# Product keys: which engine makes the pair sums of the last of eight heads

## The chip, the core and the metric

The kernel runs on one core of one Trainium2 chip. The metric is the device time of one execution in microseconds (us); the median of several runs counts.

## What is computed

The program is a stack of eight residual layers over x of 8 x 256 x 128 (2048 tokens of 128 channels); each adds its result to x, after a layer norm. The change touches the fourth, a product-key memory, which the reference writes so (cut):

```python
xn = (x - mean) * rsqrt(var + EPS) * bn_gamma + bn_beta           # over all tokens
q = (xn @ w_q.T).reshape(b, s, 2, NH, KD).transpose(2, 0, 1, 3, 4)
sim = einsum('pbnhd,hkpd->pbnhk', q, keys_p)                       # 2 halves x 8 heads x 32 keys
scores, idx = top_k(sim, K)                                        # K = 8 of each half
all_scores = scores[0][..., :, None] + scores[1][..., None, :]     # 8 x 8 pair sums
sc, pk = top_k(all_scores, K)                                      # the best 8 pairs
hmid = sigmoid(sc) * gelu(einsum('bnd,bnhkd->bnhk', inputs, down[indices]))
out = einsum('bnhk,bnhkd->bnd', hmid, up[indices])
```

A pair (i, j) of key indices names row 32 i + j of the tables `down` and `up`, so only the first 1024 rows are in play.

## The kernel before, in words

The tokens lie in 16 tiles of 128 (one token a partition). Each layer is a block in which every engine has its own instruction list; semaphores order them. Nothing is gathered in the product-key layer: for each of the eight heads the kernel writes out all 32 x 32 = 1024 pair sums of a token, and a threshold, the eighth best pair sum, decides which of them count.

Per tile n the work goes like this (function `product_keys`):

- **Half scores.** ScalarE applies the batch norm (`batch_normed`, L1495), TensorE multiplies by the folded query and key weights (`halves`, L1566), ScalarE copies the 512 half scores into one of two SBUF buffers `Ssb` (`store_s`, L1502). It does so for tile n+1 in the middle of tile n, after the sigmoid of head 3.
- **Pair sums.** GpSimd adds, head by head, the two halves into `A[h]`, 128 x 1024 fp32 in SBUF (L1541). One set of eight buffers `A` serves all tiles, so the sum of head h must wait until head h of the tile before has been turned by TensorE (semaphore `g_turned`), and all wait for `s_stored`. The semaphore `added` counts the sums.
- **Selection** (`picks`). VectorE finds the best 8 of each half with 16 max instructions (L1431), forms the 64 candidate sums of each head in one 128 x 512 addition (L1434; this is the "candidate sum"), and takes the best 8 of each head (L1438). It then adds the output of tile n-2 to x (`add_out`, L1452) and multiplies the turned gates of tile n-1 by the gelu values (`weigh`, the masking product, L1447).
- **Gates.** For head h ScalarE takes the sigmoid of all pair sums into one of two PSUM buffers `SG` (L1508), and VectorE multiplies it by the comparison of the pair sum with the threshold, in place in `A[h]` (L1463; these are the eight "products" of a tile). Its pair sums and thresholds come from SBUF, the sigmoid from PSUM.
- **Turn.** TensorE transposes the 1024 gates of each head in eight 128 x 128 pieces and adds the heads up in PSUM (`turn`, L1572).
- **Output.** TensorE multiplies the masked values by `up` (`output`, L1582). Beside this it projects x by `down` for the next block of four tiles (`project`, L1559), and ScalarE applies gelu (L1490).

The order on each engine is written out by hand in the `step` functions; the first four tiles are written out, the others run in a loop. ScalarE's order in a tile is: sigmoids 0 to 3, the store of the next tile's half scores, sigmoids 4 to 7, batch norm, two gelus. Sigmoid h waits for GpSimd's sum of its head and, through `g_ready`, for product h-2. The DMA queues are idle in this layer.

Of the kernel before, what the change touches and what calls it, by code (L numbers as in the profile page):

```python
# [20 lines left out]
ALU = mybir.AluOpType  # L21
# [19 lines left out]
NH, NK = 8, 32  # L41
# [30 lines left out]
def known(n, least):  # L72

    return not isinstance(n, int) or n >= least


def run_tiles(eng, step):


    for n in range(TPB):  # L80
        step(n, n, 0)
    with eng.Fori(1, NB - 1) as i:
        for r in range(TPB):
            step(i * TPB + r, r, i)
    for n in range(NT - TPB, NT):
        step(n, n % TPB, NB - 1)
# [90 lines left out]
def over(ap, axis, n):  # L177

    ap = ap.unsqueeze(axis)
    shape = list(ap.shape)  # L180
    shape[axis] = n
    return ap.broadcast_to(shape)
# [52 lines left out]
def norm_scalar(act, k, nm, first=None, high=None):  # L235

    act.wait_ge(nm.var_ready, 1)
    act.activation(k.mom[:, 6, :], k.mom[:, 4, :], ACT.Sqrt, bias=k.eps[:, 0:1],
                   scale=1.0 / D).then_inc(nm.std_ready, 1)
    if nm.turn:  # L240
        if first:
            first()
        for b in range(NB):
            act.wait_ge(nm.xt_turned, b + 1)
            act.activation(k.XT[:, bass.ts(b, BLK)], k.PS[:, b, :], ACT.Copy).then_inc(nm.xt_ready, 1)
            if high:
                high(act, b)
# [1117 lines left out]
def product_keys(k):  # L1365
# [8 lines left out]
    s = lambda what: k.sem(f"l1f_{what}")  # L1374
# [2 lines left out]
    bn_var, bn_std, bn_ready = s("bn_var"), s("bn_std"), s("bn_ready")  # L1377
    z_ready, z_stored = s("z_ready"), s("z_stored")
    xb_ready, s_ready, s_stored = s("xb_ready"), s("s_ready"), s("s_stored")
    added, sig_ready, g_ready, g_turned = s("added"), s("sig_ready"), s("g_ready"), s("g_turned")  # L1380
    m_ready, out_ready, out_added = s("m_ready"), s("out_ready"), s("out_added")

# [21 lines left out]
    def pair_scores(r, h):  # L1404
        s0 = over(Ssb[r][:, bass.ts(h, NK)], 2, NK)
        s1 = over(Ssb[r][:, bass.ts(NH + h, NK)], 1, NK)
        return A[h].rearrange("p (a b) -> p a b", a=NK), s0, s1

    with nc.Block() as block:

        @block.vector
        def _(dve):
            own = Tally(dve, vec)
            norm_vector(dve, k, nm, own)

            for q in range(NB):
                dve.wait_ge(nm.xt_ready, q + 1)
                own.mark(dve.bn_stats(bn[:, bass.ts(q, 6)], k.XT[:, bass.ts(q, BLK)]))
            own.wait()
            dve.bn_aggr(mv, bn[:, 0:24]).then_inc(bn_var, 1)  # L1420
            dve.wait_ge(bn_std, 1)
            own.settle(dve.reciprocal(brstd[:, 0:1], bstd[:, 0:1]))
            own.settle(dve.tensor_tensor(scale[:, 0:1], brstd[:, 0:1], k.col("gamma"), ALU.mult))
            own.settle(dve.tensor_tensor(tmp[:, 0:1], scale[:, 0:1], mv[:, 0:1], ALU.mult))
            dve.tensor_tensor(shift[:, 0:1], k.col("beta"), tmp[:, 0:1], ALU.subtract).then_inc(bn_ready, 1)

            def picks(n, r):
                dve.wait_ge(s_stored, n + 1)
                dve.sem_inc(paced, 1)
                for j in range(2 * NH):  # L1430
                    own.mark(dve.max(t8[:, j, :], Ssb[r][:, bass.ts(j, NK)]))  # L1431
                own.wait()

                own.settle(dve.tensor_tensor(cand.rearrange("p (h a b) -> p h a b", h=NH, a=8),  # L1434
                                             over(t8[:, 0:NH, :], 3, 8), over(t8[:, NH:, :], 2, 8), ALU.add))
                dve.sem_inc(paced, 1)
                for h in range(NH):
                    own.mark(dve.max(v8[:, h, :], cand[:, bass.ts(h, 64)]))  # L1438
                own.wait()

            def weigh(n, r, q):

                dve.wait_ge(g_turned, (n + 1) * NH)
                dve.wait_ge(z_stored, (q + 1) * 8)
                if known(n, 2):
                    dve.wait_ge(out_ready, n - 1)
                dve.tensor_tensor(M[r].rearrange("p (c t) -> p c t", c=8), gt.rearrange("p (c t) -> p c t", c=8),  # L1447
                                  zT[:, :, bass.ts(n, P)], ALU.mult).then_inc(m_ready, 1)

            def add_out(n):  # L1450
                dve.wait_ge(out_ready, n + 1)
                dve.tensor_tensor(k.X[:, n, :], k.X[:, n, :], PS[:, OUT, 0:D], ALU.add).then_inc(out_added, 1)  # L1452

            def step(n, t, q):
                r = t % 2
                picks(n, r)
                if known(n, 2):
                    add_out(n - 2)
                if known(n, 1):
                    weigh(n - 1, 1 - r, q if t else q - 1)  # L1460
                for h in range(NH):
                    dve.wait_ge(sig_ready, n * NH + h + 1)
                    dve.scalar_tensor_tensor(A[h], A[h], v8[:, h, 7:8], SG[h % 2], ALU.is_ge,  # L1463
                                             ALU.mult).then_inc(g_ready, 1)

            per = 2 * NH + 1 + NH
            for n in range(TPB):
                step(n, n, 0)
            with dve.Fori(1, NB) as i:
                own.enter(i - 1, TPB * per)  # L1470
                for t in range(TPB):
                    step(i * TPB + t, t, i)
            own.leave(NB - 1)
            add_out(NT - 2)
            weigh(NT - 1, 1, NB - 1)
            add_out(NT - 1)

        @block.scalar
        def _(act):
            act.wait_ge(wf_ready, 1)  # L1480
            act.activation(Wf, PS[:, WF, :], ACT.Copy).then_inc(wf_stored, 1)
            norm_scalar(act, k, nm)
            act.wait_ge(bn_var, 1)
            act.activation(bstd[:, 0:1], mv[:, 1:2], ACT.Sqrt, bias=k.eps[:, 0:1]).then_inc(bn_std, 1)
            act.wait_ge(bn_ready, 1)

            def gelu(m, c, q):

                act.wait_ge(z_ready, m + 1)
                act.activation(zT[:, c, bass.ts(q, BLK)], PS[:, Z + c % 2, :], ACT.Gelu).then_inc(z_stored, 1)  # L1490

            def batch_normed(n, r):
                if known(n, 2):
                    act.wait_ge(s_ready, n - 1)
                act.activation(xb[r], k.XT[:, bass.ts(n, P)], ACT.Identity, bias=shift[:, 0:1],  # L1495
                               scale=scale[:, 0:1]).then_inc(xb_ready, 1)

            def store_s(n, r):
                act.wait_ge(s_ready, n + 1)
                if known(n, 2):  # L1500
                    act.wait_ge(added, (n - 1) * NH)
                act.activation(Ssb[r], PS[:, SP, :], ACT.Copy).then_inc(s_stored, 1)  # L1502

            def sigmoid(n, h):
                act.wait_ge(added, n * NH + h + 1)
                if known(n, 1) or h >= 2:
                    act.wait_ge(g_ready, n * NH + h - 1)
                act.activation(SG[h % 2], A[h], ACT.Sigmoid).then_inc(sig_ready, 1)  # L1508

            def step(n, t, q):  # L1510
                r = t % 2
                for h in range(4):
                    sigmoid(n, h)
                if not isinstance(n, int) or n + 1 < NT:
                    store_s(n + 1, 1 - r)
                for h in range(4, NH):
                    sigmoid(n, h)
                if not isinstance(n, int) or n + 2 < NT:
                    batch_normed(n + 2, r)
                if not isinstance(n, int) or n + TPB < NT:  # L1520
                    for c in (2 * t, 2 * t + 1):
                        gelu(n * 2 + 8 + c % 2, c, q + 1)

            batch_normed(0, 0)
            batch_normed(1, 1)
            store_s(0, 0)
            for c in range(8):
                gelu(c, c, 0)
            run_tiles(act, step)

        @block.gpsimd
        def _(pool):
            k.clear_last(pool)

            def step(n, t, q):
                r = t % 2
                pool.wait_ge(s_stored, n + 1)
                for h in range(NH):
                    if known(n, 1):
                        pool.wait_ge(g_turned, (n - 1) * NH + h + 1)  # L1540
                    pool.tensor_tensor(*pair_scores(r, h), ALU.add).then_inc(added, 1)  # L1541
            run_tiles(pool, step)
# [634 lines left out]
```

## Time and profile before

| | us |
|---|---|
| median of 3 runs | 1546.37 (1543.95 to 1548.54) |
| the profiled execution, its own time | 1538.79 |
| span of its instructions | 1537.1 |
| busy: TensorE / VectorE / ScalarE / GpSimd | 1341.4 / 1054.2 / 936.5 / 878.9 |
| the product-key layer's tiles in it, first pair sum to last output add | about 387.7 to 647.8 |

The times in the rows below count from the start of the span. In a timeline a line is "start, duration, engine, line, operation, output <- inputs, shapes, count", and several like instructions in a row are one line; what stands in brackets is the idle time ahead of it and what ended it. PE is TensorE, PEld its weight loads, DVE VectorE, ACT ScalarE, POOL GpSimd. PEclk is the share of full speed that TensorE's clock was granted. RA holds the buffers `A`, RW the half scores and the candidates.

### The profile page before, as it was taken

The numbers are of one execution on the slowest core, as the hardware profiler recorded it, in microseconds if no ns is written. First come the engines' busy times: TensorE is split into PE (matmuls) and PEld (weight loads), VectorE is DVE, ScalarE is ACT, GpSimd is POOL, SyncE is SP. The second block draws the span as 40 slices with busy tenths as digits, with TensorE's granted clock in tenths as the row PEclk, the third lists the DMA queues.
The fourth block names the chain that finished last, engine by engine and source line by source line (L and its number), as shares of the span: only waits on it lengthen the run. The fifth ranks groups of instructions, "written<-read, shape, count | busy, mean of one in ns | idle before, by whom it ended". The sixth has DMA issues, their size and how long they took to land. (4 is left out here: it accounts for less than half of the span.)

```text
span 1537.1 us, 25078 instructions
## 1 busy us (share of the span) xinstructions
PE 1341.4 (87%) x8116; PEld 1040.6 (68%) x8116; DVE 1054.2 (69%) x2126; ACT 936.5 (61%) x1435; POOL 878.9 (57%) x619
## 2 busy tenths in 40 slices
PE   9789999797888887789489999998898349999998
PEld 8767777465466666646368887885787338787786
DVE  5534444597699999889756666673666766666665
ACT  4467787553787876477246765556665327555554
POOL 4168888300899999532047776661345128666655
PEclk9689999898899999899689999999999769999999
DMA  6021110000000000030044435332000135443442
GB/s 250 1 63 43 42 48 27 2 2 1 1 1 1 1 0 0 26 142 2 1 136 127 127 123 178 129 124 113 2 1 1 55 78 130 122 130 123 129 120 86
DMA packets 51561, 103.31 MB, mean 67 GB/s; under 512 B 6248, under 2 KB 10928, under 8 KB 49936
## 3 DMA queue, kind: packets, MB, share of 16 engines
q1 hardware_dynamic: 51472, 102.17, 21.6%
q8 instruction: 50, 0.82, 0.2%
q14 instruction: 39, 0.32, 0.1%
HBM read 99.99 MB, written 2.16 MB: 66 GB/s over the span
## 5 line engine op out<-in xcount | busy, mean ns | idle before, releaser
L1541 POOL TENSOR_TENSOR RA<-RW 128x1024 f32<-128x1024 f32 x128 | 246.7, 1965 | 86.1 <-ACT RW L1502 86.1
L881 ACT ACTIVATE PS<-PS 128x512 f32<-128x512 f32 (+1 forms) x260 | 151.1, 582 | 215.3 <-PE PS L677 214.6
L974 POOL TENSOR_TENSOR l3f_hid_rest<-RW,l3f_hid_high 128x512 fp32r<-128x512 f32 x132 | 170.5, 1292 | 141.3 <-ACT l3f_hid_high L873 141.3
L974 POOL TENSOR_TENSOR l2f_hid_rest<-RW,l2f_hid_high 128x512 fp32r<-128x512 f32 x128 | 165.3, 1292 | 136.9 <-ACT l2f_hid_high L873 136.9
L974 POOL TENSOR_TENSOR l0f_hid_rest<-RW,l0f_hid_high 128x512 fp32r<-128x512 f32 x128 | 165.2, 1292 | 64.7 <-ACT l0f_hid_high L873 56.4
L934 DVE TENSOR_TENSOR RW<-RW,PS 128x512 f32<-128x512 f32 (+1 forms) x260 | 178.7, 687 | 11.7 <-DVE RW L929 0.9
L1572 PE MATMUL PS<-identf,RA 128*128 128x128 f32 x1024 | 139.8, 287 | 37.0 <-DVE RA L1463 33.1
L1572 PEld LDWEIGHTS PS<-identf,RA 128*128 128x128 f32 x1024 | 118.1, 147 | 72.6 <-DVE RA L1463 69.3
L1463 DVE SCALAR_TENSOR_TENSOR RA<-RA,RW,PS 128x1024 f32<-128x1024 f32 x128 | 157.0, 1277 | 11.0 <-ACT PS L1508 10.4
L1508 ACT ACTIVATE PS<-RA 128x1024 f32<-128x1024 f32 x128 | 130.1, 1026 | 54.3 <-DVE RA L1463 51.8
L934 DVE TENSOR_TENSOR RW<-RD,PS 128x512 f32<-128x512 f32 x128 | 87.9, 687 | 108.3 <-ACT PS L881 99.9
L929 DVE TENSOR_TENSOR RW<-RB,PS 128x512 f32<-128x512 f32 x128 | 88.0, 688 | 92.1 <-PE PS L677 83.1
L929 DVE TENSOR_TENSOR RW<-RD,PS 128x512 f32<-128x512 f32 x128 | 87.9, 687 | 86.0 <-PE PS L677 73.9
L881 ACT ACTIVATE PS<-PS,cols 128x512 f32<-128x512 f32 x128 | 84.6, 662 | 37.6 <-PE PS L677 37.3
L675 PE MATMUL PS<-l3f_x_high,l3f_first_high 128*128 (+1 forms) x224 | 88.9, 397 | 9.7 <-DVE RW L934 9.6
L676 PE MATMUL PS<-l3f_x_rest,l3f_first_high 128*128 (+1 forms) x224 | 87.7, 392 | 0.0
L677 PE MATMUL PS<-l3f_x_high,l3f_first_rest 128*128 (+1 forms) x224 | 87.7, 391 | 0.0
L873 ACT ACTIVATE l3f_hid_high<-RW 128x512 fp32r<-128x512 f32 x132 | 82.4, 624 | 7.5 <-DVE RW L934 7.5
L873 ACT ACTIVATE l2f_hid_high<-RW 128x512 fp32r<-128x512 f32 x128 | 79.9, 624 | 8.8 <-DVE RW L934 8.7
L873 ACT ACTIVATE l0f_hid_high<-RW 128x512 fp32r<-128x512 f32 x128 | 79.8, 623 | 5.1 <-DVE RW L934 5.1
L274 PE MATMUL PS<-identf,XN 128*128 128x128 f32 x128 | 31.2, 398 | 39.5 <-DVE XN L231 39.5
L675 PE MATMUL PS<-l0f_hid_high,l0f_w_high 128*128 128x512 f32 x128 | 56.8, 443 | 6.1 <-POOL l0f_hid_rest L974 6.1
(339 smaller groups left out, 3346.4 us busy)
## 6 DMA issues: line engine op xcount, KB each, us to landing
RD<-l2f_kept SPq DMA_DIRECT2D x128, 256.0 KB, 3.5
RB<-l3f_kept SPq DMA_DIRECT2D x128, 256.0 KB, 3.7
RD<-l0f_kept SPq DMA_DIRECT2D x32, 256.0 KB, 3.1
RA<-in_w SPq DMA_DIRECT2D x2, 2048.0 KB, 10.0
RA<-in_wg SPq DMA_DIRECT2D x2, 1024.0 KB, 9.7
RA<-in_wu SPq DMA_DIRECT2D x2, 1024.0 KB, 11.7
RA<-in_wd SPq DMA_DIRECT2D x2, 1024.0 KB, 13.6
RC<-in_wg SPq DMA_DIRECT2D x1, 2048.0 KB, 8.5
```

Source lines behind the costliest of these rows:

```text
L675: pe.matmul(out, wh, xh, start=start, stop=False)
L676: pe.matmul(out, wh, xl, start=False, stop=False)
L677: return pe.matmul(out, wl, xh, start=False, stop=stop)
L873: act.activation(e.HIGH[c][0:st.rows, :], e.HID[c][0:st.rows, :], ACT.Copy).then_inc(e.rounded, 1)
L881: act.activation(gate, gate, e.func, bias=st.bias).then_inc(e.acted, 1)
L929: dve.tensor_tensor(product, factor, up, ALU.mult).then_inc(e.multiplied, 1)
L934: dve.tensor_tensor(place(e.HID, c, st), factor, PS[rows, e.GATE + c % e.gates, :], ALU.mult).then_inc(e.weighted, 1)
L974: pool.tensor_tensor(rest, hid, high, ALU.subtract).then_inc(e.hidden_ready, 1)
L1463: dve.scalar_tensor_tensor(A[h], A[h], v8[:, h, 7:8], SG[h % 2], ALU.is_ge, ALU.mult).then_inc(g_ready, 1)
L1508: act.activation(SG[h % 2], A[h], ACT.Sigmoid).then_inc(sig_ready, 1)
L1541: pool.tensor_tensor(*pair_scores(r, h), ALU.add).then_inc(added, 1)
L1572: mm = pe.matmul(gt[:, bass.ts(c, P)], A[h][:, bass.ts(c, P)], k.identf[:], start=(h == 0 and c % 4 == 0), stop=(h == NH - 1), is_transpos ...
```

## The change

The pair sums of the last head (h = 7) are taken off GpSimd's list, which makes seven per tile. VectorE makes them instead, between the products of heads 3 and 4 of the same tile, behind a wait for the turn of the previous tile's last head. A new semaphore `added_last` counts them; ScalarE's sigmoid 7 and its store of half scores wait for it, and the counts of `added` go by seven. The instruction is the same `tensor_tensor` addition with the same operands.

```diff
--- before.py
+++ after.py
@@ -1377,6 +1377,7 @@
     bn_var, bn_std, bn_ready = s("bn_var"), s("bn_std"), s("bn_ready")
     z_ready, z_stored = s("z_ready"), s("z_stored")
     xb_ready, s_ready, s_stored = s("xb_ready"), s("s_ready"), s("s_stored")
+    added_last = s("added_last")
     added, sig_ready, g_ready, g_turned = s("added"), s("sig_ready"), s("g_ready"), s("g_turned")
     m_ready, out_ready, out_added = s("m_ready"), s("out_ready"), s("out_added")
 
@@ -1459,6 +1460,10 @@
                 if known(n, 1):
                     weigh(n - 1, 1 - r, q if t else q - 1)
                 for h in range(NH):
+                    if h == NH // 2:
+                        if known(n, 1):
+                            dve.wait_ge(g_turned, n * NH)
+                        dve.tensor_tensor(*pair_scores(r, NH - 1), ALU.add).then_inc(added_last, 1)
                     dve.wait_ge(sig_ready, n * NH + h + 1)
                     dve.scalar_tensor_tensor(A[h], A[h], v8[:, h, 7:8], SG[h % 2], ALU.is_ge,
                                              ALU.mult).then_inc(g_ready, 1)
@@ -1498,11 +1503,15 @@
             def store_s(n, r):
                 act.wait_ge(s_ready, n + 1)
                 if known(n, 2):
-                    act.wait_ge(added, (n - 1) * NH)
+                    act.wait_ge(added, (n - 1) * (NH - 1))
+                    act.wait_ge(added_last, n - 1)
                 act.activation(Ssb[r], PS[:, SP, :], ACT.Copy).then_inc(s_stored, 1)
 
             def sigmoid(n, h):
-                act.wait_ge(added, n * NH + h + 1)
+                if h < NH - 1:
+                    act.wait_ge(added, n * (NH - 1) + h + 1)
+                else:
+                    act.wait_ge(added_last, n + 1)
                 if known(n, 1) or h >= 2:
                     act.wait_ge(g_ready, n * NH + h - 1)
                 act.activation(SG[h % 2], A[h], ACT.Sigmoid).then_inc(sig_ready, 1)
@@ -1535,7 +1544,7 @@
             def step(n, t, q):
                 r = t % 2
                 pool.wait_ge(s_stored, n + 1)
-                for h in range(NH):
+                for h in range(NH - 1):
                     if known(n, 1):
                         pool.wait_ge(g_turned, (n - 1) * NH + h + 1)
                     pool.tensor_tensor(*pair_scores(r, h), ALU.add).then_inc(added, 1)
```

## Rows read from the trace of the kernel before

**Rows 1.** Busy time by stretch: twelve tiles, then one tile.

```profile
core 0: us, PE busy (x) PEld busy (x) DVE busy (x) ACT busy (x) POOL busy (x), PEclk, DMA share, GB/s
440.00:631.00 191.00, 157.30 (x1048) 119.24 (x1046) 184.03 (x448) 144.95 (x161) 191.00 (x100) 0.98 0.00 1
507.74:523.36 15.62, 13.16 (x87) 9.57 (x86) 14.92 (x37) 12.60 (x14) 15.62 (x9) 1.00 0.00 1
```

**Rows 2.** Waits of VectorE in the same 191 us: total us, times, longest.

```profile
DVE RW L1438 <- DVE RW L1434: 1.7, 11, 0.2
DVE RA L1463 <- ACT PS L1508: 1.5, 10, 0.2
DVE X L1452 <- DVE RW L1438: 0.8, 3, 0.3
```

**Rows 3.** Timeline of one tile, VectorE and ScalarE: start us, us, what.

```profile
507.74 4.90 DVE L1463 SCALAR_TENSOR_TENSOR RA<-RA,RW,PS 128x1024 f32<-128x1024 f32 x4
511.26 0.58 ACT L1502 ACTIVATE RW<-PS 128x512 f32<-128x512 f32 x1
517.62 1.58 DVE L1431 MAX8 RW<-RW 128x8 f32<-128x32 f32 x16
519.23 1.07 DVE L1434 TENSOR_TENSOR RW<-RW 128x512 f32<-128x512 f32 x1
521.83 0.29 DVE L1452 TENSOR_TENSOR X<-X,PS 128x128 f32 x1 [0.25 <-DVE RW L1438]
523.36 4.90 DVE L1463 SCALAR_TENSOR_TENSOR RA<-RA,RW,PS 128x1024 f32<-128x1024 f32 x4
```

**Rows 4.** GpSimd sums (L1541) and VectorE's candidate sum (L1434): instructions in ns, then timelines.

```profile
L1541 POOL TENSOR_TENSOR RA<-RW x128: 1900/1910/2375, 387.7 to 633.7; 128x1024 f32<-128x1024 f32 x128
L1434 DVE TENSOR_TENSOR RW<-RW x16: 753/1028/1492, 389.4 to 627.1; 128x512 f32<-128x512 f32 x16
387.67 1.91 POOL L1541 TENSOR_TENSOR RA<-RW 128x1024 f32<-128x1024 f32 x1 [84.84 <-ACT RW L1502]
389.35 0.77 DVE L1434 TENSOR_TENSOR RW<-RW 128x512 f32<-128x512 f32 x1
425.33 1.92 POOL L1541 TENSOR_TENSOR RA<-RW 128x1024 f32<-128x1024 f32 x1
426.31 1.49 DVE L1434 TENSOR_TENSOR RW<-RW 128x512 f32<-128x512 f32 x1
427.19 2.38 POOL L1541 TENSOR_TENSOR RA<-RW 128x1024 f32<-128x1024 f32 x1
430.43 1.27 DVE L1463 SCALAR_TENSOR_TENSOR RA<-RA,RW,PS 128x1024 f32<-128x1024 f32 x1
```

**Rows 5.** Larger additions with two SBUF inputs: a group (mean ns), then a timeline.

```profile
L1033 DVE TENSOR_TENSOR RB<-RB 128x1024 f32<-128x1024 f32 x1 | 1.2, 1224 | 0.0
661.79 1.27 POOL L1268 TENSOR_TENSOR RB<-RB,vmask 128x512 f32<-128x512 f32 x1 [26.19 <-DVE RB L1170]
662.16 3.05 DVE L1174 TENSOR_TENSOR X<-X,rows 128x2048 f32<-128x2048 f32 x1
663.02 3.32 POOL L1268 TENSOR_TENSOR RB<-RB,vmask 128x512 f32<-128x512 f32 x1
```

**Rows 6.** Timeline of the first tile and of the last tile's products.

```profile
400.12 9.97 DVE L1463 SCALAR_TENSOR_TENSOR RA<-RA,RW,PS 128x1024 f32<-128x1024 f32 x8 [8.74 <-ACT PS L1508]
403.65 0.58 ACT L1502 ACTIVATE RW<-PS 128x512 f32<-128x512 f32 x1
404.31 1.92 POOL L1541 TENSOR_TENSOR RA<-RW 128x1024 f32<-128x1024 f32 x1 [1.21 <-ACT RW L1502]
631.07 9.77 DVE L1463 SCALAR_TENSOR_TENSOR RA<-RA,RW,PS 128x1024 f32<-128x1024 f32 x8
```

**Rows 7.** Busy time of a stretch with a lower granted clock, columns as above.

```profile
414.80:424.70 9.90, 8.56 (x58) 7.86 (x58) 9.75 (x10) 7.85 (x10) 9.90 (x6) 0.83 0.01 2
```

## The prediction

> **What bounds the kernel now.** The busy times by stretch come first. Over 191 us in the middle of the product-key stage, 12.4 tiles, GpSimd is busy for all 191.00 us and VectorE for 184.03, 96% [rows 1]. TensorE and ScalarE are at 82% and 76%. The reader is to see two engines at the limit, not one. A GpSimd sum takes 1910 ns in the median, and its neighbours overlap slightly: one starts at 425.33, its successor is recorded from 427.19, 1.86 later [rows 4]. Eight of them and one delay of 0.45 us, explained below, make 15.3 to 15.4 us. The first product of tile 0 starts at 400.12 and that of tile 15 at 631.07 [rows 6]: 230.95 / 15 = 15.40 us a tile. So GpSimd paces the stage, and its pace for one sum is (15.40 - 0.45) / 8 = 1.87 us.
>
> The waits come second: how much room has VectorE? In the same 191 us it waits 1.5 us for ScalarE's sigmoid, 1.7 us for its own previous result and 0.8 us in front of the output add [rows 2]. Per tile that is a third of a microsecond, and the 1.7 is a latency that nothing here removes. The timeline of one tile, third, shows VectorE's order with no other hole: eight products from 507.74, the selection from 517.62, the candidate sum at 519.23, the next tile's products at 523.36 [rows 3].
>
> **What is moved.** Per tile one 128x1024 sum leaves GpSimd (1.87 us of its pace) and comes to VectorE, between the fourth and fifth product; sixteen in all. No DMA is touched.
>
> *Its bare cost on VectorE.* This stage has no such sum there. The nearest row is the same operation, shape and type, both inputs in SBUF, in another layer: 1224 ns [rows 5]. Neighbours overlap a little, so one adds about 1.1 us.
>
> *Its wait.* The stage already holds one VectorE operation with two SBUF inputs, the candidate sum of 128x512 (L1434). It should cost the same each time, yet takes 753 to 1492 ns [rows 4]. The GpSimd sums beside it explain this. At 389.35 a GpSimd sum is running that ends at 387.67 + 1.91 = 389.58; VectorE ends at 390.12, 0.54 later. At 426.31 the running sum ends at 427.25, and VectorE ends at 427.80, 0.55 later [rows 4]. VectorE's operation gets nowhere until the running GpSimd sum ends, then needs 0.55 us. The next GpSimd sum, recorded from 427.19, takes 2.38 us instead of 1.91: it waits in turn, which is the 0.45 above. A larger case agrees: a 128x2048 add that starts at 662.16 under a GpSimd operation ending at 663.06 ends at 665.21, 2.15 later, and the next GpSimd operation takes 3.32 us where the one before took 1.27 [rows 5]. From 512 to 2048 elements the part behind the wait goes from 0.55 to 2.15, so 1024 elements take 0.55 + 512 x 1.60 / 1536 = 1.08 us. The products have one SBUF input and don't show this: four take 4.90 us beside GpSimd, eight 9.77 in the last tile, half of it without GpSimd [rows 3, 6].
>
> The Trainium skill bears on this: the page "Advanced Engine Details and Errata", section "VectorE Performance Modes", says that the second Vector SBUF port is shared, so that GpSimd and two-port Vector instructions block each other, and the page "VectorE: DVE Perf Modes", section "Mode 2×_2P — use both read ports for one tensor", says that tensor_tensor cannot use that mode. Taken to the letter nothing would block here, and the time would be the first rival's. The rows above speak against the letter. "GPSIMD Engine Reference", section "Key points", counts two SBUF inputs as a case too; with that the trace agrees.
>
> *Where GpSimd stands when the new sum comes.* Count from a tile's first product, t = 0. ScalarE stores the next tile's half scores from 511.26 to 511.84, until t = 4.10 [rows 3]. If GpSimd is idle then, it starts 0.08 us later (ScalarE ends at 404.23, GpSimd starts at 404.31 [rows 6]), so its first sum runs from 4.18 to 6.09. VectorE's fourth product ends at 4.90 [rows 3]. So in every tile the new sum starts under that first sum, waits until 6.09 and ends at 6.09 + 1.08 = 7.17: about 2.3 us of VectorE's time, not 1.1. Behind it in the queue stand products 4 to 7 and the next selection; TensorE's turns and ScalarE's sigmoids 6 and 7 wait for these.
>
> *What follows in the tile.* The remaining products take 4.9 us, to 12.0; the selection starts at 11.95 and the candidate sum 1.61 later (517.62 to 519.23 [rows 3]), at 13.56. GpSimd's second sum was held up and ends 1.77 after VectorE lets go (the one from 427.19 ends at 429.57, VectorE had ended at 427.80 [rows 4]), at 8.94; the third, fourth and fifth end at 10.81, 12.68 and 14.55. The candidate sum therefore waits for the fifth and ends at 14.55 + 0.55 = 15.10. From its end to the next tile's first product it is 3.06 us in one tile (520.30 to 523.36 [rows 3]), which includes the 0.25 of wait in front of the output add, and 2.63 where the candidate sum was longest (427.80 to 430.43 [rows 4]). I take 2.85. The period is 15.10 + 2.85 = 17.95 us.
>
> Is GpSimd idle when I said so? Its seven sums start at 4.18 and need 7 x 1.87 + 0.45 + about 1.0 (the hold by the moved sum: midway by size between 0.45 and 3.32 - 1.27 = 2.05), to 18.7; its next start is at 17.95 + 4.18 = 22.1. Yes, for 3.4 us. Its work is then hidden; so is the 13.16 us of TensorE and the 12.60 of ScalarE in a tile [rows 1].
>
> *New waits, costed at nothing.* VectorE's wait for the turn of the previous tile's last head has been passed by its masking product, earlier in the same queue; without it VectorE would stand for one turn, about the 1.2 us of a product. ScalarE's sigmoid 7 waits for the moved sum (done at 7.2), but is not due before product 5 is done (about 9.6); any lateness beyond that would add to the period in full. ScalarE's store of half scores waits for sums of the tile before last, long done; a late one would shift GpSimd's start by as much.
>
> **Sum.** Fifteen periods x (17.95 - 15.40) = 38.3; the last tile's moved sum finds GpSimd done and costs about 1.1; together +39.4 us. The profiled execution took 1538.79 us, so 1578 by its own time. The median of the runs shown, 1546.37, lies 7.6 above it; there I expect 1546.4 + 39.4 = 1586.
>
> **Rivals.**
> 1. *The moved sum doesn't wait for GpSimd* (its access pattern differs, or it falls between sums). A tile then pays 1.1 less the 0.12 us of sigmoid wait [rows 2]: 15 x 1.0 + 1.1 = 16, so 1562. For it: 1224 ns in another layer [rows 5]. Against: all the rows beside GpSimd. 0.08.
> 2. *Faster: GpSimd alone paces, VectorE takes the sum in idle time.* Place: the whole period. Price: 7 x 1.87 + 0.45 = 13.5 us a tile, or 14.5 with the hold, so 0.9 to 1.9 less, about -20 in all: 1526. It decides if VectorE has 1.1 us free per tile. For it: GpSimd's 191.00 of 191.00. Against: VectorE's idle 6.97 us, 0.56 a tile [rows 1], half of it fixed. 0.02. The Trainium skill has the rule behind it ("GPSIMD Engine Reference", section "Engine selection": elementwise work on a tile belongs on VectorE, GpSimd being about twice as slow); 1910 against 1224 ns agrees in direction.
> 3. *VectorE loses to a second GpSimd sum as well*: +1.87 a tile, 1586 + 28 = 1614. No row shows it. 0.03.
> 4. *TensorE's granted clock falls* with the longer pauses. It is 1.00 now, the level of 2.4 GHz [rows 1]; were every tile at 1.2 GHz, TensorE's 13.16 us would come to 26.3 at most, and to no loss at least: 0 to 15 x 8.4 = 125 us. A stretch granted 0.83 still kept VectorE 9.75 of 9.90 us busy [rows 7], so I stay near the lower end, 0.5 a tile: 1594. 0.03.
>
> **Numbers.** The forecast has 0.84. Its own ends: a period from 17.6 (tail 2.5) to 18.2 (tail 3.1) gives +34 to +43, and the runs shown differ by 4.6 us, so 1577 to 1592. Widened to rival 4 and somewhat below: 1574 to 1594, which leaves out rivals 1 to 3. A difference of 0.3% (4.6 us) is about what a measurement of this kernel can tell from none. Faster gets 0.02 (rival 2), the same 0.01 (between rivals 1 and 2), slower 0.97.
>
> **What would show it.** Right: sixteen new VectorE sums of some 2.3 us, the last near 1.2; the GpSimd sum after each near 2.9 us; candidate sums near 1.5; tiles 17.9 us apart; GpSimd idle some 3.4 us a tile until the half scores are stored. New sums of 1.2 us would show rival 1, of 4 us rival 3, tiles under 15.4 us apart rival 2, a granted clock near 0.5 rival 4. If GpSimd still ran without a pause, the phase that I counted from would be wrong.

## The result, and the profile after

The changed kernel is slower: 1582.72 us in the median of four runs (1580.27 to 1584.09) against 1545.16 us before, in four runs as well (1540.02 to 1548.54; the table ahead has three of them), a ratio of 1.0256 with a 95% interval of 1.0227 to 1.0285. That is 37.6 us more, where 39.4 had been summed. The profiled execution took 1580.27 us.

The span and the busy times of the profile's page, after:

```profile
span 1578.3 us, 25062 instructions
...
PE 1358.0 (86%) x8116; PEld 1050.5 (67%) x8116; DVE 1095.9 (69%) x2142; ACT 936.0 (59%) x1435; POOL 863.7 (55%) x603
```

Busy time by stretch in the product-key layer after, the columns as in [rows 1]: 191 us, then one tile.

```profile
core 0: us, PE busy (x) PEld busy (x) DVE busy (x) ACT busy (x) POOL busy (x), PEclk, DMA share, GB/s
460.00:651.00 191.00, 145.19 (x902) 108.93 (x902) 186.42 (x392) 126.24 (x141) 156.08 (x76) 0.95 0.00 0
523.96:542.16 18.20, 13.58 (x87) 9.50 (x86) 17.66 (x37) 12.54 (x14) 14.76 (x8) 1.00 0.00 1
```

GpSimd, busy for 191.00 of 191 us before, is busy for 156.08; VectorE, 184.03 before, for 186.42. Read as shares, VectorE is now at 98% with less done per microsecond. Its waits and those of GpSimd in the same stretch say little about it (total us, times, longest):

```profile
DVE RW L1439 <- DVE RW L1435: 1.5, 10, 0.2
DVE X L1453 <- DVE RW L1439: 0.8, 3, 0.3
POOL RA L1550 <- ACT RW L1508: 34.9, 10, 3.6
```

The wait for the sigmoid [rows 2] is gone, and GpSimd now waits some 3.5 us a tile (34.9 / 10) for the half scores. The new loss stands in no list of waits, for it lies inside the instructions. The groups, after (duration in ns: least, median, most; then first and last start): the moved sum, the candidate sum, GpSimd's sums, the products.

```profile
L1466 DVE TENSOR_TENSOR RA<-RW x16: 1218/2396/2466, 403.5 to 673.0; 128x1024 f32<-128x1024 f32 x16
L1435 DVE TENSOR_TENSOR RW<-RW x16: 766/1602/1631, 388.0 to 663.7; 128x512 f32<-128x512 f32 x16
L1550 POOL TENSOR_TENSOR RA<-RW x112: 1899/1910/2895, 386.3 to 667.1; 128x1024 f32<-128x1024 f32 x112
L1468 DVE SCALAR_TENSOR_TENSOR RA<-RA,RW,PS x128: 1267/1273/1282, 398.7 to 677.8; 128x1024 f32<-128x1024 f32 x128
```

The products are as before. The moved sum takes 2396 ns in the median, twice its least; the candidate sum 1602, which was 1028 [rows 4]; the longest GpSimd sum 2895, which was 2375. One tile after, VectorE, ScalarE and GpSimd in order of time, the counterpart of [rows 3]:

```profile
523.96 4.85 DVE L1468 SCALAR_TENSOR_TENSOR RA<-RA,RW,PS 128x1024 f32<-128x1024 f32 x4
527.42 0.58 ACT L1508 ACTIVATE RW<-PS 128x512 f32<-128x512 f32 x1
528.19 1.92 POOL L1550 TENSOR_TENSOR RA<-RW 128x1024 f32<-128x1024 f32 x1 [3.44 <-ACT RW L1508]
528.73 2.46 DVE L1466 TENSOR_TENSOR RA<-RW 128x1024 f32<-128x1024 f32 x1
530.07 2.89 POOL L1550 TENSOR_TENSOR RA<-RW 128x1024 f32<-128x1024 f32 x1
531.11 4.84 DVE L1468 SCALAR_TENSOR_TENSOR RA<-RA,RW,PS 128x1024 f32<-128x1024 f32 x4
535.88 1.57 DVE L1432 MAX8 RW<-RW 128x8 f32<-128x32 f32 x16
536.66 1.91 POOL L1550 TENSOR_TENSOR RA<-RW 128x1024 f32<-128x1024 f32 x1
537.49 1.63 DVE L1435 TENSOR_TENSOR RW<-RW 128x512 f32<-128x512 f32 x1
539.27 1.11 DVE L1439 MAX8 RW<-RW 128x8 f32<-128x64 f32 x8 [0.15 <-DVE RW L1435]
542.16 1.27 DVE L1468 SCALAR_TENSOR_TENSOR RA<-RA,RW,PS 128x1024 f32<-128x1024 f32 x1
```

GpSimd's first sum starts at 528.19, 0.19 us after ScalarE has stored the half scores, and ends at 530.11. VectorE's sum starts under it at 528.73 and ends at 531.19, 1.08 us after it. GpSimd's second sum, recorded from 530.07, takes 2.89 us. The candidate sum starts at 537.49 under a GpSimd sum that ends at 538.57, and ends 0.55 us later. The first tile and the last, the counterpart of [rows 6]:

```profile
398.66 2.47 DVE L1468 SCALAR_TENSOR_TENSOR RA<-RA,RW,PS 128x1024 f32<-128x1024 f32 x2 [8.66 <-ACT PS L1517]
668.17 4.90 DVE L1468 SCALAR_TENSOR_TENSOR RA<-RA,RW,PS 128x1024 f32<-128x1024 f32 x4
672.99 1.22 DVE L1466 TENSOR_TENSOR RA<-RW 128x1024 f32<-128x1024 f32 x1
```

From 398.66 to 668.17 it is 15 periods of 17.97 us. In the last tile GpSimd has nothing left to do, and there the sum takes 1.22 us.

### The profile page after: what moved, and what is told of

Read it like the earlier page. It is cut to its first block and busy times, and to the rows that moved or that the text cites. A ratio compares the mean times of both kernels' runs of the same rounds, so it can differ in the third digit from the quotient of the medians.

```text
span 1578.3 us, 25062 instructions
## 1 busy us (share of the span) xinstructions
PE 1358.0 (86%) x8116; PEld 1050.5 (67%) x8116; DVE 1095.9 (69%) x2142; ACT 936.0 (59%) x1435; POOL 863.7 (55%) x603
## 5 line engine op out<-in xcount | busy, mean ns | idle before, releaser
L1550 POOL TENSOR_TENSOR RA<-RW 128x1024 f32<-128x1024 f32 x112 | 231.9, 2103 | 135.6 <-ACT RW L1508 135.6
L1581 PE MATMUL PS<-identf,RA 128*128 128x128 f32 x1024 | 149.5, 298 | 60.9 <-DVE RA L1468 54.7
L1581 PEld LDWEIGHTS PS<-identf,RA 128*128 128x128 f32 x1024 | 124.2, 153 | 102.1 <-DVE RA L1468 102.1
```

The source lines that it names most:

```text
L1581: mm = pe.matmul(gt[:, bass.ts(c, P)], A[h][:, bass.ts(c, P)], k.identf[:], start=(h == 0 and c % 4 == 0), stop=(h == NH - 1), is_transpos ...
```

## The experiments

Each of the seven kernels is compared with the kernel before on the same chip. The period is the distance of the first products of tile 0 and tile 15, divided by 15; "held" is the longest GpSimd sum.

| kernel | period us | moved sum ns | candidate sum ns | held ns | time against before |
|---|---|---|---|---|---|
| before | 15.40 | none | 1028 | 2375 | 1 |
| changed | 17.97 | 2396 | 1602 | 2895 | 1.0256 |
| 1 moved sum goes first | 17.11 | 1218 | 1937 | 2370 | 1.0156 (1.0123 to 1.0189) |
| 2 moved sum two products earlier | 16.98 | 1216 | 1812 | 2365 | 1.0184 (1.0153 to 1.0215) |
| 3 candidates half in PSUM | 17.17 | 2392 | 687 | 2895 | 1.0198 (1.0170 to 1.0225) |
| 4 no eighth sum | 15.15 | none | 842 | 2367 | 0.9987 (0.9965 to 1.0009) |
| 5 the edits of 2 and 3 together | 15.97 | 1218 | 686 | 1925 | 1.0065 (1.0040 to 1.0090) |
| 6 before, candidates half in PSUM | 15.12 | none | 687 | 1922 | 0.9988 (0.9968 to 1.0008) |
| 7 before, candidate sum on GpSimd | 15.35 | none | 1093 on GpSimd | none | 1.0005 (0.9986 to 1.0024) |

The intervals of experiments 1, 2 and 3 overlap, so their times don't put these three in an order; what follows goes by the periods and by the durations of the instructions. Each period is read from one traced execution.

### 1. The moved sum goes first

```diff
                 pool.wait_ge(s_stored, n + 1)
+                if known(n, 1):
+                    pool.wait_ge(added_last, n)
                 for h in range(NH - 1):
```

> The changed kernel, but GpSimd starts a tile's sums only when VectorE has made its own sum of the tile before. The same instructions in the same places on VectorE; only who has the port first is turned round. Theory (VectorE's two-input operation waits for the running GpSimd sum): the moved sum takes 1.2 us instead of 2.4, products end at 10.85 after a tile's first instead of 12.0, the selection's candidate sum starts at 12.4 and waits for GpSimd's fourth sum, which now ends at 13.6, so it takes 1.8 us; period 17.1 us instead of 17.97, time about 1570 beside 1583 for the changed kernel. Rival (the sum is slow on VectorE by itself, since its inputs are read with a step of zero): the moved sum stays at 2.4 us and the time at 1583 or above. Rival (GpSimd's work binds in the changed kernel): holding GpSimd back by 1.9 us a tile lengthens the period by as much, 1610.

Measured: 1569.08 us in the median (1564.58 to 1578.89). The groups of the moved sum and of the candidate sum:

```profile
L1466 DVE TENSOR_TENSOR RA<-RW x16: 1215/1218/1220, 414.8 to 671.4; 128x1024 f32<-128x1024 f32 x16
L1435 DVE TENSOR_TENSOR RW<-RW x16: 770/1937/2016, 398.6 to 661.9; 128x512 f32<-128x512 f32 x16
```

And from its timeline the moved sum, the GpSimd sum behind it and the next candidate sum:

```profile
534.02 1.22 DVE L1466 TENSOR_TENSOR RA<-RW 128x1024 f32<-128x1024 f32 x1
535.49 1.92 POOL L1552 TENSOR_TENSOR RA<-RW 128x1024 f32<-128x1024 f32 x1 [3.57 <-PE PS L1583]
541.54 2.02 DVE L1435 TENSOR_TENSOR RW<-RW 128x512 f32<-128x512 f32 x1
```

VectorE's list is unchanged to the instruction, and the sum sits in the same place; that GpSimd begins behind it and not ahead of it makes 1218 ns out of 2396 in all sixteen tiles. So the second half of its time was a wait for GpSimd, and not its way of reading. (The bracket names TensorE as what ended GpSimd's idle time. By the edit GpSimd waits for VectorE's sum, which ends at 535.24, 0.25 us ahead of it.) GpSimd, held back by some 2 us a tile, lengthened nothing: the rival that has GpSimd pace the changed kernel falls. The candidate sum, at 541.54, now meets another GpSimd sum at another point and takes 2.02 us. The period is 17.11 where 17.1 was expected.

### 2. The moved sum two products earlier

```diff
-                    if h == NH // 2:
+                    if h == 2:
```

> The changed kernel with VectorE's sum between products 1 and 2 instead of 3 and 4, where GpSimd should be idle (its last sum ends about 0.8 us after a tile's first product, its next starts at 4.2; the sum comes at 2.4). Theory of the port: the sum takes 1.2 us, ScalarE's store still ends at 4.1, GpSimd runs as before, the candidate sum starts at 12.4, now under GpSimd's fifth sum, which ends at 13.57, so it takes 1.75 us; period 17.05 us instead of 17.97, time about 1569. Rival (slow by itself): 2.4 us in the new place too, period and time as in the changed kernel, 1583.

Measured: 1570.25 us (1568.74 to 1575.25). The moved sum, the candidate sum and GpSimd's sums:

```profile
L1466 DVE TENSOR_TENSOR RA<-RW x16: 1214/1216/1219, 407.6 to 662.3; 128x1024 f32<-128x1024 f32 x16
L1435 DVE TENSOR_TENSOR RW<-RW x16: 770/1812/1892, 393.4 to 655.4; 128x512 f32<-128x512 f32 x16
L1550 POOL TENSOR_TENSOR RA<-RW x112: 1897/1912/2365, 391.8 to 658.8; 128x1024 f32<-128x1024 f32 x112
```

In GpSimd's pause the sum takes 1216 ns and holds nothing up: the longest GpSimd sum is back at 2365 ns, the one behind the candidate sum. Same operation, same operands, another moment. What is left over the kernel before is the bare sum and a candidate sum that waits longer than in the changed kernel (1812 ns).

### 3. The candidates half in PSUM

```diff
+    t8b = PS[:, 2, 0:64].rearrange("p (n j) -> p n j", j=8)
...
+                    if j == NH and known(n, 1):
+                        dve.wait_ge(g_ready, n * NH)
+                        dve.sem_inc(paced, 1)
-                    own.mark(dve.max(t8[:, j, :], Ssb[r][:, bass.ts(j, NK)]))
+                    own.mark(dve.max(t8[:, j, :] if j < NH else t8b[:, j - NH, :], Ssb[r][:, bass.ts(j, NK)]))
...
-                                             over(t8[:, 0:NH, :], 3, 8), over(t8[:, NH:, :], 2, 8), ALU.add))
+                                             over(t8[:, 0:NH, :], 3, 8), over(t8b, 2, 8), ALU.add))
+                dve.sem_inc(cand_made, 1)
...
+                if h == 0:
+                    act.wait_ge(cand_made, n + 1)
```

> The changed kernel, but the best 8 of each second half are written to PSUM, so that the candidate sum has one input in SBUF and one in PSUM. Theory of the port (two SBUF inputs are the trigger): the candidate sum takes 0.65 to 0.7 us in every tile instead of 1.6, no GpSimd sum is held up by it any more (none of 2.36 us, but one of 2.9 a tile stays), the moved sum stays at 2.4; period 17.0 instead of 17.97, time about 1568. Rival (any VectorE operation beside GpSimd waits, or the candidate sum is slow by its pattern): it stays at 1.6 us and the time at 1583.

Measured: 1573.12 us (1571.94 to 1575.79). The moved sum, the candidate sum and GpSimd's sums, then one candidate sum and the GpSimd sum that runs beside it:

```profile
L1472 DVE TENSOR_TENSOR RA<-RW x16: 1220/2392/2462, 409.9 to 667.4; 128x1024 f32<-128x1024 f32 x16
L1440 DVE TENSOR_TENSOR RW<-RW,PS x16: 686/687/689, 393.3 to 659.0; 128x512 f32<-128x512 f32 x16
L1558 POOL TENSOR_TENSOR RA<-RW x112: 1897/1907/2895, 391.6 to 661.9; 128x1024 f32<-128x1024 f32 x112
503.69 1.91 POOL L1558 TENSOR_TENSOR RA<-RW 128x1024 f32<-128x1024 f32 x1
504.52 0.69 DVE L1440 TENSOR_TENSOR RW<-RW,PS 128x512 f32<-128x512 f32 x1
```

With one input in PSUM the candidate sum takes 686 to 689 ns in all sixteen tiles, beside GpSimd sums that run through it: the one shown starts at 504.52 and is done at 505.21, 0.39 us before the GpSimd sum under which it started. The moved sum, still with two inputs in SBUF, keeps its 2392 ns and still holds a GpSimd sum to 2895. So it is the pair of SBUF inputs that makes a VectorE operation wait here. The period came to 17.17, 0.17 over the expectation: part of that is that from the end of the candidate sum to the next product some 0.1 us more passes than in the changed kernel.

### 4. No eighth sum

```diff
-                    if h == NH // 2:
-                        if known(n, 1):
-                            dve.wait_ge(g_turned, n * NH)
-                        dve.tensor_tensor(*pair_scores(r, NH - 1), ALU.add).then_inc(added_last, 1)
...
-                else:
-                    act.wait_ge(added_last, n + 1)
+                elif not known(n, 1):
+                    act.wait_ge(added_last, 1)
...
                     pool.tensor_tensor(*pair_scores(r, h), ALU.add).then_inc(added, 1)
+                if not known(n, 1):
+                    pool.tensor_tensor(*pair_scores(r, NH - 1), ALU.add).then_inc(added_last, 1)
```

> The first half of the change alone: GpSimd makes seven sums a tile and nobody makes the eighth (left out: the pair sums of head 7 in tiles 1 to 15; its sigmoid then reads what the buffer holds). It tells what taking a sum off GpSimd is worth. Theory (VectorE was full before): GpSimd is idle 1.5 us a tile, VectorE paces at 15.2 us a tile instead of 15.40, its candidate sum takes about 0.8 us; time 3 to 4 us under before, about 0.998 of it. Rival (GpSimd alone paced the kernel before): the period falls by a whole sum to 13.5 us, time 28 us under before, 0.98 of it.

Measured: 1540.86 us (1535.31 to 1543.57), no difference from before that this many runs can tell. The candidate sum, GpSimd's sums, and what GpSimd waited for in 140 us (9.2 tiles):

```profile
L1435 DVE TENSOR_TENSOR RW<-RW x16: 758/842/919, 387.9 to 622.3; 128x512 f32<-128x512 f32 x16
L1545 POOL TENSOR_TENSOR RA<-RW x112: 1898/1912/2367, 386.2 to 626.6; 128x1024 f32<-128x1024 f32 x112
POOL RA L1545 <- ACT RW L1503: 16.2, 10, 1.8
```

Taking a whole sum from the engine that was never idle shortens the period by 0.25 us, from 15.40 to 15.15, and then GpSimd waits 1.8 us a tile. With the rest as it is, this is all that taking the sum off GpSimd can gain, and it needs VectorE to make the sum at no cost.

### 5. Both edits: no wait for GpSimd at all

The edits of experiments 2 and 3 together.

> The two edits of the second and the third experiment together in the changed kernel: the sum between products 1 and 2, and half of the candidates' inputs in PSUM. No VectorE operation then waits for a GpSimd sum. Theory (the move costs VectorE its bare time, even without any wait at the port, since VectorE was full): sum 1.22 us, candidate sum 0.69, period 16.0 us against 15.40 before, so +9 and 1 for the last tile: 1.006 times before. Rival (the wait at the port was the whole loss): period 15.4 or less, time as before or under it.

Measured: 1554.33 us (1550.76 to 1556.06). The moved sum, the candidate sum and GpSimd's sums:

```profile
L1472 DVE TENSOR_TENSOR RA<-RW x16: 1217/1218/1219, 405.6 to 645.2; 128x1024 f32<-128x1024 f32 x16
L1440 DVE TENSOR_TENSOR RW<-RW,PS x16: 686/686/689, 392.1 to 639.3; 128x512 f32<-128x512 f32 x16
L1558 POOL TENSOR_TENSOR RA<-RW x112: 1901/1912/1925, 390.4 to 642.3; 128x1024 f32<-128x1024 f32 x112
```

Neither engine holds up the other any more: the moved sum takes 1218 ns, the candidate sum 686, and no GpSimd sum more than 1925. The move still costs 0.57 us a tile over the kernel before, and 0.65 % of the time. So the wait was most of the loss but not all of it.

### 6. The kernel before, candidates half in PSUM

The edit of experiment 3 on the kernel before.

> The kernel before (eight sums on GpSimd) with half of the candidates' inputs in PSUM. Theory: the candidate sum takes 0.69 us instead of 1.03 in the mean, no GpSimd sum is held up, GpSimd's pace becomes 8 x 1.87 = 14.96 us, VectorE's about 15.0 to 15.1; period 15.1 against 15.40, time about 5 us under before, 0.997 of it. Rival (the port costs nothing where GpSimd paces): period 15.4, same time.

Measured: 1541.69 us (1535.01 to 1544.66), ratio 0.9988 with an interval that reaches to 1.0008. Busy time in 140 us, columns as in [rows 1], and GpSimd's sums:

```profile
core 0: us, PE busy (x) PEld busy (x) DVE busy (x) ACT busy (x) POOL busy (x), PEclk, DMA share, GB/s
460.00:600.00 140.00, 117.25 (x781) 88.12 (x780) 134.05 (x319) 111.07 (x124) 138.33 (x75) 0.99 0.00 1
L1549 POOL TENSOR_TENSOR RA<-RW x128: 1897/1912/1922, 388.0 to 629.4; 128x1024 f32<-128x1024 f32 x128
```

The period falls to 15.12 as expected, and no GpSimd sum is held up; yet 0.28 us in 15 periods is 4 us, and the runs don't tell it from nothing. It is the fastest complete kernel here by its period, and not one that can be called faster.

### 7. The opposite exchange

```diff
+    def two_heads(r, g):
+        both = RA[:, bass.ts(g, 2 * NE)].rearrange("p (h a b) -> p h a b", h=2, a=NK)
...
-                own.settle(dve.tensor_tensor(cand.rearrange("p (h a b) -> p h a b", h=NH, a=8),
-                                             over(t8[:, 0:NH, :], 3, 8), over(t8[:, NH:, :], 2, 8), ALU.add))
+            def best_pairs(n):
+                dve.wait_ge(cand_made, n + 1)
...
-                for h in range(NH):
+                for g in range(NH // 2):
+                    if g == 2:
+                        pool.wait_ge(t8_ready, n + 1)
+                        pool.tensor_tensor(cand.rearrange("p (h a b) -> p h a b", h=NH, a=8),
...
+                    pool.tensor_tensor(*two_heads(r, g), ALU.add).then_inc(added, 1)
```

> The opposite exchange, on the kernel before: GpSimd makes the sums two heads at a time (four instructions of 128x2048, estimated at 3.2 us each from 1.91 for 1024 and 1.27 for 512 elements), and in the time saved also the candidate sum (1.3 us); VectorE has no operation with two SBUF inputs left in a tile, and makes the masking product while GpSimd adds the candidates. Theory: VectorE's tile is 9.9 us of products, 1.6 of first selection, 1.2 of masking product, 1.4 of second selection, 0.4 of output add: 14.5 us; GpSimd's 4 x 3.15 + 1.27 = 13.9 fits; time 13 us under before, 0.991 of it. Rival (a GpSimd sum of two heads takes twice one, 3.8 us): GpSimd's tile is 16.5 us, time 16 us over before, 1.010.

Measured: 1545.68 us (1537.80 to 1547.37), as before. GpSimd's sums of two heads and its candidate sum:

```profile
L1551 POOL TENSOR_TENSOR RA<-RW x64: 3633/3664/3684, 389.8 to 635.3; 128x2048 f32<-128x2048 f32 x64
L1546 POOL TENSOR_TENSOR RW<-RW x16: 1066/1093/1110, 397.0 to 630.7; 128x512 f32<-128x512 f32 x16
523.76 14.47 POOL L1551 TENSOR_TENSOR RA<-RW 128x2048 f32<-128x2048 f32 x4
```

The two-head sum takes 3664 ns, and the four in a row 14.47 us; with the candidate sum GpSimd's tile is 15.4 us again. VectorE's own work came to 13.7 us a tile (124.69 us busy in 140), under the 14.5 worked out, and it now waits where it had not: for GpSimd's candidate sum, and ahead of the masking product (total us, times, longest, in 240 us):

```profile
DVE RW L1442 <- POOL RW L1546: 13.1, 14, 1.4
DVE RW L1451 <- DVE RW L1434: 6.6, 15, 0.6
```

That is 19.7 us of VectorE's time in some 15 tiles. The expectation failed in one number, the estimate of 3.2 us for two heads, and with it the gain.

## Why the prediction was right, point by point

- **Two engines at the limit.** Shown by experiment 4: with GpSimd relieved of a sum and VectorE given nothing, the period stays at 15.15. Rival 2, which read GpSimd's full busy time as the only bound, had 13.5 to 14.5.
- **The bare cost of 1.1 us.** The last tile's 1.22 us, overlap included, and experiment 5: from 15.12 (experiment 6, the same without the move) to 15.97 it is 0.85 us a tile. Of the 0.25 that are missing to 1.1, 0.15 are the wait for the sigmoid ahead of product 4 (1.5 us in ten waits, [rows 2]), which disappears behind the sum. The other 0.1 is not explained.
- **The wait.** The sum of 6.09 + 1.08 = 7.17 was right to 0.1 us: the moved sum ends at t = 531.19 - 523.96 = 7.23 in the tile shown, 1.08 behind GpSimd's sum, and at 7.12 to 7.28 in all fifteen. It takes 2396 ns in the median where 7.17 - 4.90 = 2.27 us followed from the working, chiefly because it starts at t = 4.76 to 4.83 and not at 4.90; the earlier start only lengthens the wait. In eight of the fifteen tiles GpSimd starts 0.16 to 0.19 rather than 0.08 us after the store, as in the tile shown. The 1.08 and the 0.55 behind it hold without exception: in this layer, in the traces of before, after and experiments 1 to 4, 110 VectorE sums with two SBUF inputs start under a GpSimd sum, and every one ends 0.55 us (512 elements) or 1.08 us (1024) after it. Rival 1 falls with experiments 1 and 2, which show the same sum at 1.2 us as soon as GpSimd is not running.
- **What is late next.** The candidate sum was to meet GpSimd's fifth sum and take 1.54 us; it took 1602 ns. Experiment 3 prices its whole wait: 17.97 to 17.17, 0.8 us a tile. The kernel before already paid 0.28 of that (15.40 to 15.12, experiment 6), so some 0.5 of the 2.57 us, a fifth of the loss, came from an instruction that the diff doesn't touch. With the 1.18 us by which the moved sum's 2396 ns exceed 1218, and the 0.85 of bare cost, it makes 2.55 of the 2.57. The GpSimd sum behind the moved one was to take 2.9 us; it takes 2.89.
- **GpSimd idle** for 3.4 us a tile: 34.9 us in ten waits. VectorE never lost to two GpSimd sums in a row (rival 3): no moved sum exceeds 2466 ns.
- **TensorE's clock** (rival 4): granted 0.95 over the 191 us, against 0.98 before, and 1.00, the level of 2.4 GHz, in the tile shown. No wait of VectorE for TensorE appears, so it cost nothing that the profile shows in this stage.
- **The sum.** 17.95 us a tile was forecast, 17.97 measured. The profiled spans differ by 41.2 us; 15 x 2.57 + 1.1 = 39.6 of that lies in these sixteen tiles, and the rest in layers that the change doesn't touch. The medians differ by 37.6; the forecast of 1586 stood on a median of before that was 1.2 above the later one. The steps hold one by one, in the mean of the fifteen tiles: the candidate sum starts at t = 13.52 (13.56 forecast) and ends at 15.12 (15.10), and from there to the next tile it is 2.85 (2.85). That the last, chosen between 2.63 and 3.06, met the mean so closely is luck; the mean of the same stretch in the trace of before, also 2.85, would have given it with a reason.

The Trainium skill's page "Advanced Engine Details and Errata", section "VectorE Performance Modes", names only two-port Vector instructions as the ones that block GpSimd and are blocked by it. Taken to the letter it would have given the first rival's 1562; the runs gave 1582.72. The Trainium skill's page "GPSIMD Engine Reference", section "Key points", counts two SBUF inputs as a case of contention as well. The runs agree with that: the candidate sum takes 1602 ns with two SBUF inputs in the changed kernel and 687 with one in experiment 3.

What was not tried: the moved sum itself with one input in PSUM, since no PSUM bank is free at its place. How the chip decides who goes first is not shown, only that VectorE's operation always came directly behind the GpSimd sum that was running, and the next GpSimd sum behind VectorE's.

## What to carry to other kernels

Before an elementwise operation goes from GpSimd to VectorE, look at where in the cycle GpSimd is running: in these traces a VectorE addition with two SBUF inputs waits for the GpSimd addition under way, and the next GpSimd addition waits for it. The wait is inside the instruction's duration, so that here a busy share of 98% holds 2 us of it in 18; a like operation whose duration varies from time to time in the trace of before is the sign, and putting one input into PSUM (the candidate sum, 1602 to 687 ns) or the operation into GpSimd's pause (the moved sum, 2396 to 1216 ns) took the wait away. And an engine that is never idle need not be the only bound: leaving its work out altogether, as in experiment 4, tells what moving it can bring at best.

## What the runs showed of the hardware that was not expected

- Two heads in one GpSimd instruction hardly save anything: 3664 ns for 2048 elements, 1910 for 1024, 1093 for 512. The 1.27 us of a 128x512 multiplication by GpSimd [rows 5], on which the estimate of 3.2 us for two heads had rested, is another operation with other operands and was no measure of it.
- One and the same candidate sum takes 0.75 to 2.02 us with two SBUF inputs, by the moment at which it starts under a GpSimd sum; with one input in PSUM 686 to 689 ns beside such sums.
